# A four-part graph network kernel: setup and slot stage joined in one block, with the input loads, the weights and the clearing on other queues

## The reference

```
x = layernorm(x + gat(x, src, dst, 3 attention layers))          # L0
x = layernorm(x + edge_mlp(x[src], edge_attr), mean over dst)    # L1
x = layernorm(x + relational(x, edge_type, 8 weights))           # L2
x = layernorm(x + gcn_pos_neg(x, edge_weight, 2 layers))         # L3
```

## Time and profile before

| | us |
|---|---|
| median of three runs | 3882.38 |
| lowest and highest | 3877.11, 3891.00 |
| the profiled execution | 3880.98 |
| its span, first to last instruction | 3879.3 |
| VectorE busy | 2985.1 (77%) |
| TensorE busy | 2903.3 (75%) |
| ScalarE busy | 1393.6 (36%) |
| mean granted TensorE clock | 0.893 |

### The profile page before, as it was taken

One profiled execution on the slowest core, in us unless ns is written; L12 is line 12 of the kernel. 1 busy time (PEld: TensorE's weight loads), 2 busy tenths in 40 slices (PEclk: granted clock), 3 DMA queues, 4 the chain that ended last, 5 costly groups with the idle time before them and its releaser, 6 DMA issues. The chain is left out here.

```text
span 3879.3 us, 77817 instructions
## 1 busy us (share of the span) xinstructions
PE 2903.3 (75%) x25843; PEld 2103.0 (54%) x25926; DVE 2985.1 (77%) x6871; ACT 1393.6 (36%) x2725; POOL 1210.0 (31%) x1109
## 2 busy tenths in 40 slices
PE   0158888888407707707769999699999699979994
PEld 0135555555302202202259999456565499969994
DVE  6877777778589999999977777555555599968887
ACT  0024444444304405405459999233333210010000
POOL 0034445455238737636600000155555100000000
PEclk9998888889659959959979999799999799989997
DMA  7936565556458828728847675122222144323331
GB/s 304 378 98 179 147 182 163 166 161 182 148 162 289 260 83 283 253 88 277 258 157 219 216 230 168 47 66 69 66 65 66 37 107 108 106 55 89 91 90 37
DMA packets 444431, 596.30 MB, mean 154 GB/s; under 512 B 82795, under 2 KB 331434, under 8 KB 444052
## 3 DMA queue, kind: packets, MB, share of 16 engines
q1 hardware_dynamic: 395623, 450.37, 39.4%
q0 software_dynamic: 34592, 68.90, 5.9%
q10 hardware_dynamic: 13836, 72.12, 4.8%
HBM read 354.68 MB, written 230.75 MB: 151 GB/s over the span
## 5 line engine op out<-in xcount | busy, mean ns | idle before, releaser
L1213 PE MATMUL psum<-a_probs,z 128*65 128x512 f32 (+1 forms) x1050 | 436.3, 555 | 134.1 <-DVE a_probs L1111 133.4
L914 POOL DMA_INDIRECT slots<-bc_rec,idx x400 | 392.1, 980 | 399.8 <-ACT bc_rec L874 300.8
L1806 DVE TENSOR_SCALAR rp_hot_dst<-rp_ramp,slot_key 128x696 bf16<-128x696 f16 x900 | 298.8, 401 | 230.3 <-PE psum L1950 230.3
L535 POOL DMA_INDIRECT slots<-h,idx x256 | 336.7, 1315 | 310.8 <-DMA h<-recs 239.8
L1147 ACT ACTIVATE a_tops<-a_tops,a_s_low 128x512 f32<-128x512 f32 (+2 forms) x300 | 283.0, 946 | 271.8 <-DVE a_tops L1102 254.7
L1213 PEld LDWEIGHTS psum<-a_probs,z 128*65 128x65 f32 x1050 | 122.5, 139 | 443.5 <-DVE a_probs L1111 275.3
L1783 POOL DMA_INDIRECT rp_fetch<-piece_rows,slot_row x283 | 279.2, 987 | 247.5 <-PE psum L1950 191.1
L1102 DVE SCALAR_TENSOR_TENSOR a_tops<-table,a_s_rest,big 128x512 f32<-128x512 f32 (+2 forms) x300 | 307.7, 1028 | 2.8 <-DMA big<-shift_rows 2.8
L1111 DVE SCALAR_TENSOR_TENSOR a_probs<-a_tops,a_counts 128x512 f32<-128x512 f32 (+2 forms) x300 | 289.8, 967 | 11.4 <-ACT a_tops L1147 7.6
L1878 ACT ACTIVATE rp_msg<-psum 128x192 bf16<-128x192 f32 (+1 forms) x456 | 176.2, 387 | 310.3 <-PE psum L1924 275.6
L793 PE MATMUL psum<-acc 128*128 128x512 f16 x1000 | 194.1, 339 | 115.3 <-issue 64.2
(11 more groups left out here) (452 smaller groups left out, 6613.7 us busy)
## 6 DMA issues: line engine op xcount, KB each, us to landing
slots<-big ACTq DMA_DIRECT2D x60, 1012.5 KB
ep_rec<-slots SPq DMA_DIRECT2D x60, 1012.5 KB, 6.0
a_counts<-edge_counts SPq DMA_DIRECT2D x75, 538.5 KB
a_counts<-edge_counts SPq DMA_DIRECT2D x150, 256.0 KB
a_counts<-edge_counts SPq DMA_DIRECT2D x75, 512.0 KB
edge_counts<-bc_counts SPq DMA_DIRECT2D x12, 3125.0 KB
hot_rows<-ep_hot_src SPq DMA_DIRECT2D x300, 96.0 KB
sp_hot_src<-hot_rows SPq DMA_DIRECT2D x300, 96.0 KB
```

The costliest lines, as they stand in the source:

```text
L535: pool.indirect_dma_start(k.slots, bass.IndirectOffsetOnAxis(k.idx[:, at:at + 1], 0), self.rows[y][:, t, :], None).then_inc(self.scattered ...
L914: pool.indirect_dma_start(k.slots, bass.IndirectOffsetOnAxis(k.idx[:, first + t:first + t + 1], 0), rec[:, j, t, :], None).then_inc(scatte ...
L1213: last = nc.tensor.matmul(sums[:, a:b], k.z[:, s, 0:D + 1], probs[:, a:b], start=s == 0, stop=True, skip_group_check=True)
L1806: v.tensor_scalar(hot_dst[:, q % HOT_SLOTS, :], ramp[:, :], k.slot_key[:, q:q + 1], None, ALU.is_equal)\
```

## The change

`setup` is gone as a block, and its work stands in `edge_slots`.

- SP: the four edge inputs come first, then, once `big` is cleared, the 60 clearing stores.
- ScalarE: it issues the load of `x` and the 36 loads of weights, waits for the edge inputs, makes two fields of `meta` that VectorE made before (L398, L399), serves the seven batches, and then makes the 25 masks in two steps each: a square of (tile number - key), and a Relu of (1 - square).
- VectorE: it does the work of `setup` first. `score_weights` stands behind the step `diag` and waits for all the weights. The mask instruction is gone from its loop.
- TensorE: the seven batches stand ahead of the carry product.
- GpSimd: `all_rows` is made last.

```diff
+                sp.wait_ge(cleared, 1)
...
-                    act.dma_start(to.rearrange("(p s) f -> p (s f)", p=P), flat[:, 0:per]).then_inc(k.filled, 16)
+                    sp.dma_start(to.rearrange("(p s) f -> p (s f)", p=P), flat[:, 0:per]).then_inc(k.filled, 16)
+
+            @block.scalar
+            def _(act):
+                act.dma_start(k.x[:, :, :], d["x"].rearrange("(t p) f -> p t f", p=P)).then_inc(x_in, 16)
+                for to, source in parts:
+                    act.dma_start(to, source).then_inc(weights_in, 16)
+                act.wait_ge(loaded, 4 * 16)
+                nc.scalar.activation(meta[:, 0:ET, 1], w[:, :], ACT.Relu).then_inc(marked, 1)
+                nc.scalar.activation(meta[:, 0:ET, 2], w[:, :], ACT.Relu, scale=-1.0).then_inc(marked, 1)
...
+                act.wait_ge(numbers_made, 1)
+                act.wait_ge(tails_in, NT)
+                for i in range(NT):
+                    if i >= 2:
+                        act.wait_ge(chosen, i - 1)
+                    nc.scalar.activation(mask[:, i % 2, :], key[:, :], ACT.Square, bias=k.bin_lane[:, i:i + 1], scale=-1.0)\
+                        .then_inc(squared, 1)
+                    act.wait_ge(squared, i + 1)
+                    nc.scalar.activation(mask[:, i % 2, :], mask[:, i % 2, :], ACT.Relu, bias=k.ones[:, 0:1], scale=-1.0)\
+                        .then_inc(masked, 1)
...
                 v.memset(ones[:, :], 1.0)
-                score_weights(k, chain, w_first, w_score, 0)
-                v.memset(x_turned[D:D + 1, :], 1.0).then_inc(w_made, 1)
                 dve.wait_ge(loaded, 4 * 16)
...
-                v.tensor_scalar(meta[:, 0:ET, 1], w[:, :], 0.0, None, ALU.max)
-                v.tensor_scalar(meta[:, 0:ET, 2], w[:, :], -1.0, 0.0, ALU.mult, ALU.max)
...
                 v.tensor_scalar(diag[:, :], k.ident[:, :], top[:, 0:1], None, ALU.mult).then_inc(row_in, 1)
+                dve.wait_ge(weights_in, 16 * len(parts))
+                score_weights(k, chain, w_first, w_score, 0)
+                v.memset(x_turned[D:D + 1, :], 1.0).then_inc(w_made, 1)
...
                 for i in range(NT + 1):
-                    if i < NT:
-                        if i >= 2:
-                            dve.wait_ge(chosen, i - 1)
-                        v.tensor_scalar(mask[:, i % 2, :], key[:, :], i + 1.0, None, ALU.is_equal).then_inc(masked, 1)
...
-                pe.wait_ge(row_in, 4)
-                nc.tensor.matmul(ps_carry, link[:, :], tails[:, :], start=True, stop=True).then_inc(pe_done, 1)
+                pe.wait_ge(x_in, 16)
                 pe.wait_ge(w_made, 1)
...
                     last.then_inc(z_out, 1)
+                pe.wait_ge(row_in, 4)
+                nc.tensor.matmul(ps_carry, link[:, :], tails[:, :], start=True, stop=True).then_inc(pe_done, 1)
```

More of the change, by code:

```diff
@@ L241, in magic_round @@
     chain.link(v.tensor_scalar(out, out, -1.5 * 2.0 ** 23, None, ALU.add))
[L244 to L295, removed]
@@ L336, in edge_slots @@
         w_made, x_out, x_copied, z_out, z_taken = sem("w_made"), sem("x_out"), sem("x_copied"), sem("z_out"), sem("z_taken")
+        parts = [p for name, source in weight_sources(d).items() for p in weight_parts(k, name, source)]
         batches = [range(t, min(t + AT_ONCE, NT)) for t in range(0, NT, AT_ONCE)]
@@ L345, in _ @@
                 sp.dma_start(w[:, :], d["weight_rank"]).then_inc(loaded, 16)
-            @block.scalar
-            def _(act):
-                act.wait_ge(loaded, 4 * 16)
+                sp.wait_ge(cleared, 1)
                 per = SLOTS * FILL * REC
@@ L374, in _ @@
                                         fill=0.0, base=0, pattern=[[1, P]], channel_multiplier=-1).then_inc(made, 1)
+                nc.gpsimd.iota(k.all_rows[:, :, :], pattern=[[P, NT], [1, P]], base=1, channel_multiplier=0)
             @block.vector
@@ L378, in _ @@
                 v, chain = nc.vector, Chain(dve, step)
+                v.memset(k.big[:, :, :], 0.0).then_inc(cleared, 1)
+                v.memset(k.ones[:, :], 1.0)
+                v.memset(k.zero_rec[:, :], 0.0)
+                dve.wait_ge(lanes_made, 1)
+                v.tensor_copy(k.bin_lane[:, :], ints[:, :]).then_inc(numbers_made, 1)
+                chain.link(v.tensor_copy(bins[:, :], bins_i[:, :]))
+                magic_round(v, chain, k.bin_first[:, :], bins[:, :], 1.0 / TN, -0.496)
+                v.scalar_tensor_tensor(k.bin_first[:, :], k.bin_first[:, :], float(P - TN), bins[:, :], ALU.mult, ALU.add)
+                v.tensor_copy(k.lane[:, :], lane_i[:, :])
+                v.tensor_scalar(k.minus_lane[:, :], lane_i[:, 0:1], -1.0, None, ALU.mult)
+                v.tensor_copy(k.tile_first[:, :, :], first_i[:, :, :])
+                dve.wait_ge(diagonal_made, 1)
+                v.tensor_copy(k.ident16[:, :], k.ident[:, :])
                 v.memset(ones[:, :], 1.0)
-                score_weights(k, chain, w_first, w_score, 0)
-                v.memset(x_turned[D:D + 1, :], 1.0).then_inc(w_made, 1)
                 dve.wait_ge(loaded, 4 * 16)
@@ L2505, in program @@
             meta = early.enter_context(nc.sbuf_tensor("meta", [P, ET_LOADED, META], FP32))
-            setup(k)
             edge_slots(k, meta)
```

14 lines of the change are left out of this document (added).

## The result

| | before | after |
|---|---|---|
| median, us | 3879.74 (3870.63 to 3891.0, 4 runs) | 3921.19 (3919.02 to 3935.67, 4 runs) |
| profiled execution, us | 3880.98 | 3923.04 |
| its span, us | 3879.3 | 3921.3 |
| VectorE busy, us | 2985.1 | 2977.1 |
| ScalarE busy, us | 1393.6 | 1443.9 |

The ratio is 1.0121, 95% interval 1.0091 to 1.0151: slower, as forecast, and inside the range. The size was off: +41 us at the median and +42.1 in the profiled executions, where +63.5 was forecast.

A forecast was written before the change was run, and what follows sets the result against it. VectorE was taken to bound the slot stage, beside full DMA engines. Weights landing at 136 us plus 118.1 us gave a stage end of 254.1 instead of 190.6: +63.5 us, 3944.5 us (likeliest 3945), range 3910 to 3985.

The forecast's parts named there:

- Direction and mechanism: Slot stage: VectorE waits from 29.7 to 136 us for weights loading beside the clearing; kernel slower by 63.5 us.
- One packet for one: DMA engines alternate packets of two full queues; 428 turns of 0.294 us, weights land at 136 us; chance 0.57.
- rival 2: Bunches: one turn carries all a transfer has on an engine; weights land at 108 us, +35.5 us, 3916 us; chance 0.10.
- turn of 0.294 us: DMA engines: one clearing packet of 0.276 us plus one small packet of 0.018 us.
- by then some 45 of the 201 packets of `x` are through: Per engine, when clearing stores arrive at about 8 us: 36 beside the edge inputs, some 9 ahead; 428 turns remain.
- The start: Edge inputs issued first, at about 0.8 us; VectorE starts at 8.8 us and `diag` ends at 29.7 us.
- Behind the weights: From the weights' landing to the slot stage's end: 2.3 + 29.5 + 70.1 + 16.2, together 118.1 us.
- The rule of thumb: Shift of the slot stage's end is the landing of the weights minus 72.5 us.
- No cost behind the stage: All later blocks keep their length; only the shift of their start counts.
- Rival 1: Weights land by about 46 us; the next loads queue behind the clearing; -25.7 us, 3855 us; chance 0.18.
- Rival 3: Weights last: ScalarE's issues held back by SP's full queue, landing at 168 us; +95.5 us, 3976 us; chance 0.13.
- rival 4: ScalarE's masks late: at 3.1 us a mask the loop is as before, 8 us lost; no separate chance.

The follow-up runs named there:

- e3: The changed kernel with clearing rows of 2700 B instead of 8100 B, same bytes cleared; 3854.26 us, ratio 0.9957 to the kernel before.
- e12: The changed kernel with clearing rows of 1620 B instead of 8100 B, same bytes; 3708.12 us in one run, where the kernel before took 3712.11.
- e13: The changed kernel with TensorE's carry product ahead of the seven batches, as before the change (e7 again); 3773.97 us, ratio 1.0158.
- e5: The changed kernel with the mask instruction back in VectorE's loop and without ScalarE's two steps; 3913.68 us, ratio 1.0139.
- e11: The changed kernel itself, run again on a faster chip; 3745.77 us, where the kernel before took 3712.11, ratio 1.0089.
- e2: The changed kernel, but SP waits for all weights before it issues the clearing; 3859.27 us, ratio 0.9979.
- e8: The changed kernel, but ScalarE issues `x` and the first four weight loads, SP the other 32 ahead of the clearing; 3856.87 us, ratio 0.9986.
- e1: The changed kernel, but VectorE waits at `score_weights` for four weight loads only, for the rest behind the loop; 3876.91 us, ratio 1.0019.
- e9: e8 with all transfers of the next block (`edge_keys`) on ScalarE's queue; 3854.09 us, ratio 0.9969.
- e7: The changed kernel with TensorE's carry product ahead of the seven batches, as before the change; 3921.2 us in one run.

## Why the prediction was right in direction and wrong in size

- **Direction and mechanism: right.** VectorE stands behind a weight load for 80.75 us (106 forecast), since the clearing on SP's queue takes a turn for every row of ScalarE's.
- **One packet for one: right**, and chosen over turns by bytes on thin evidence. In the earlier trace rows the two queues together filled 32% of the engines, so neither had to give way, and equal counts there say nothing of how full queues share; that this step held was partly luck. 1097 against 1096 packets, the order of the rows, and e3 and e12, show it at three row lengths. The time alone would not have told: 3921 us lies nearer to rival 2's 3916 than to 3944.5. The turn of 0.294 us, added up from the earlier trace rows, was 0.292.
- **The step that failed: "by then some 45 of the 201 packets of `x` are through".** It took the edge inputs for a full queue and let `x` alternate with them row by row. 144 were through, because SP's queue had gaps. From the first clearing row (8.36 us) to the last weight row (111.36) there is room for 353 turns of 0.292 us instead of 428: 75 x 0.294 = 22.1 us. VectorE went on 0.8 us after that row, not 2 (1.2 us), and the shorter turn gives 0.7, less 0.4 for the later start: together 23.6 of the 23.8 us between 136 and 112.2. On average an engine had only 329 turns left (473 - 144); the last one must have had some 24 more (the trace does not tell the engines apart), and VectorE waits for the last.
- **The start** was 10.46 us, not 8.8, and `diag` ended at 31.41, not 29.7. It lay in front of a wait and cost nothing.
- **Behind the weights: 118.13 us, forecast 118.1.** `score_weights` 2.3; `live` to the end of the memset of `rank` 29.5 (114.48 to 144.01); loop 70.1 (144.01 to 214.07); tail 16.2 (to 230.29). TensorE's batches fit with some 5 us to spare, as forecast: ScalarE's last step on them starts at 137.35, and the carry is copied at 142.88. e13 shows what is lost without that, e5 what the masks bring.
- **The rule of thumb**, shift = landing - 72.5, gives 39.7 for 112.2, and the stage's end moved by 39.7 (190.57 to 230.29). In e3 it gives -16.5, and the stage's end moved by -16.5 (174.1).
- **No cost behind the stage: right** for the changed kernel. In the first pair 2 us more arose later; e11 has none of that, so I take them for scatter.
- **Rival 1 (slips through)** was wrong as to the turns, but its second half was right and is what limits e2 and e8: with the weights out of the way, the loads behind the clearing bound the next block. Its shift of -25.7 us was too large: e2 reached -12.1, since its stores are issued from 28.27 us on, not from 4.31, and SP holds the block's end besides.
- **Rival 2 (bunches)** gave 108 us for the landing, nearer than my 136, and for the wrong reason. The Trainium skill (DMA: Bandwidth & Descriptors, Queues, rings and completion order) says that an engine drains a whole packet of some 9 to 17 descriptors before it changes queues. In this kernel a transfer has some 8 rows per engine, and a whole small load could cross for one clearing store. The trace disagrees. Equal counts (1096 for 1097 in 20 us) could hide equal bunches of both queues, and the landing at 112 us is near 108; what excludes bunches is the order of the rows, one of SP's behind each of ScalarE's, and e3: a clearing store has the same bytes there, so turns by whole transfers would have left the landing near 108 us, and it moved to 56.0. The measurement decides.
- **Rival 3 (weights last)** and **rival 4 (masks late)** did not come. ScalarE was held by its own issues, though, and the prediction gives these no cost of their own; only rival 3 touches them, as a way for the weights to land last. In the changed kernel the hold ended at 83.9 us and the batches came at 115.66, so it cost nothing; in e1 it set the stage's end. The Trainium skill (DMA: Bandwidth & Descriptors, Issuing engines are not separate DMA queues) says that issuing on several engines only saves the time of the issue. Here the reverse happened, too: the issues held ScalarE for 83.9 us, where the same 36 loads and `x` had taken SP 22.2 us before (0.81 to 23.02).

**Where did the expected gain go?** Without the wait the stage would end at 31.4 + 118.1 = 149.5 us, 41 us earlier than before, and it does in e2, e8 and e9 (149.8 to 150.4). Of these 41 us the clearing takes back 23 to 29 before the node work starts (shifts of -18.4 to -12.0), because its 60 stores of 1012.5 KB take 150 us of full engines at 415 GB/s. Nothing waited for them before: the last clearing row ended at 185.4 us, 5 us ahead of the stage's end. In e2, e8 and e9 it ends at 180.4, 180.5 and 182.8 us, 30 to 33 us behind the stage's end, and the next block waits for it. The best versions run, e3 (ratio 0.9957, 17.1 us below the kernel before) and e9 (0.9969, 13.2 us), beat both kernels. They were run on different chips, and their intervals overlap, so which is the better stays open.

## What to carry to other kernels

When a short load shares the DMA engines with a bulk transfer of another queue, price it by rows: rows of the load per engine x the time of one bulk row and one of its own. Put it ahead of the bulk in the same queue, or cut the bulk's rows, and keep it off a compute engine's queue, since that engine is then held for the same turns. Before counting a stage's gain, ask what will end last then: here the queue of the bulk transfer and the engine that issues it.

## What the runs showed of the hardware that I had not expected

- After every row of one queue an engine took a row of the other, at three row lengths (8100, 2700 and 1620 B), seen row by row in the records.
- An engine issuing small loads beside full DMA engines was held 2.3 us per load (78 to 85 us for 36, in the seven traces with clearing rows of 8100 B), about as long as one load's turns, and less with shorter rows beside it (42.7 and 33.2 us).
- Four loads issued in a row on one queue left gaps in which the other queue moved 883 packets in 1 us against 30.
- The landing of the same kernel's weights moved by 5 us between two executions (112.16 and 106.82 us). In e5, e7 and e13, which differ from it only behind the weights, it was 113.86, 112.13 and 113.38.
- The chips differ by more than any change here: the kernel before took 3871 and 3867 us on two of them, and 3712 us on another. In e11, on that last one, the granted clock from 350 to 500 us was 0.98, VectorE was busy for 147.60 of 150 us, and the DMA engines moved 217 GB/s:

```profile
350.00:500.00 150.00, 137.52 (x1040) 93.30 (x1038) 147.60 (x490) 89.16 (x183) 97.03 (x101) 0.98 0.77 217
```

In the first trace of the changed kernel the same stretch has 0.86, 111.63 us and 162 GB/s. Why one chip goes faster there was not looked into. The changed kernel's ratios on the two, 1.0121 and 1.0089, have intervals that overlap.
